# A recurrent cell of 624 steps: products in three gate blocks, a one-step loop, and one input-gate piece ahead of the choice

## The reference

```
def step(carry, x_t):
    h, c = carry
    logits = concatenate([h, c, x_t]) @ W_sel.T + b_sel
    onehot = one_hot(argmax(logits), 4)
    g_all = x_t @ W_ih[s] + h @ W_hh[s] + b_ih[s] + b_hh[s]   # for each s of 4
    i, f, g, o = split(g_all of the chosen s, 4)              # 512 each
    c = sigmoid(f) * c + sigmoid(i) * tanh(g)
    h = sigmoid(o) * tanh(c)
```

## Time and profile before

| | us |
|---|---|
| median of 3 runs | 7053.28 (7048.97 to 7054.98) |
| profiled execution | 7064.35 |
| its span | 7062.7 |
| granted TensorE clock, mean over the span | 0.956 |
| PE busy | 6163.6 (87%) |
| DVE busy | 2459.5 (35%) |
| ACT busy | 1721.2 (24%) |
| the recurrent steps in the trace | 3603.5 to 6681.9 |

### The profile page before, as it was taken

How to read it: one execution, slowest core, us unless ns; L and a number is a source line. 1 busy time by engine, 2 the same in 40 slices (tenths; PEclk the granted TensorE clock), 3 DMA queues, 4 the chain that set the end, 5 groups by cost and what they waited for, 6 DMA issues and landing times. The chain is left out here.

```text
span 7062.7 us, 492288 instructions
## 1 busy us (share of the span) xinstructions
PE 6163.6 (87%) x210539; PEld 4094.5 (58%) x210539; DVE 2459.5 (35%) x11546; ACT 1721.2 (24%) x8472; POOL 928.5 (13%) x2082
## 2 busy tenths in 40 slices
PE   6856999999999999998779999999999999999852
PEld 5523555555555454554567777777777777777631
DVE  5324555555442211111233332333333332222248
ACT  0121333333333333333001111111111111111112
POOL 0011111111128810000000000000000000000003
PEclk9977999999999999999899999999999999999975
DMA  1011111111111100000232221222122221111100
GB/s 48 1 45 35 33 34 33 34 33 34 34 35 43 42 4 0 0 0 0 76 88 41 41 41 16 41 41 44 21 32 44 41 34 7 7 7 7 22 14 8
DMA packets 806866, 204.14 MB, mean 29 GB/s; under 512 B 701431, under 2 KB 766683, under 8 KB 806804
## 3 DMA queue, kind: packets, MB, share of 16 engines
q1 hardware_dynamic: 764500, 151.79, 11.3%
q0 software_dynamic: 41152, 46.42, 2.4%
q10 hardware_dynamic: 1152, 5.15, 0.2%
HBM read 174.86 MB, written 28.16 MB: 29 GB/s over the span
## 5 line engine op out<-in xcount | busy, mean ns | idle before, releaser
L1757 PE MATMUL ps_rows<-whh,h_pair 128*4 128x320 f16 x34944 | 1307.2, 299 | 85.1 <-issue 3.4
L1074 PE MATMUL ode_busy<-ode_busy_x,ode_busy_w 128*32 128x320 f16 (+4 forms) x19248 | 1247.9, 321 | 9.3 <-PEq L1010 7.1
L1757 PEld LDWEIGHTS ps_rows<-whh,h_pair 128*4 128x4 f16 x34944 | 735.5, 84 | 512.5 <-DVE h_pair L1615 154.0
L1068 PEld LDWEIGHTS ode_psa<-ode_a,ode_w2t 128*32 128x32 f32 x19968 | 397.6, 108 | 769.1 <-ACT ode_a L1183 572.3
L1627 DVE COPY gate_rows<-ps_rows_last 128x192 f32<-128x192 f32 x624 | 223.1, 358 | 1514.3 <-PE ps_rows_last L1757 1514.3
L1193 DVE SCALAR_TENSOR_TENSOR ode_part<-ode_b 128x1 f32<-128x1 f32 x624 | 112.6, 180 | 1647.9 <-ACT ode_b L1185 1647.9
L1679 ACT COPY gate_rows<-ps_rows 128x320 f32<-128x320 f32 x624 | 265.8, 426 | 1678.8 <-PE ps_rows L1757 1678.8
L1068 PE MATMUL ode_psa<-ode_a,ode_w2t 128*32 128x1 f32 x19968 | 606.8, 181 | 47.8 <-ACT ode_a L1177 43.1
L1185 ACT ACTIVATE ode_b<-ode_psa 128x1 f32<-128x1 f32 x2496 | 427.4, 171 | 814.3 <-PE ode_psa L1068 797.6
L1801 PE MATMUL ps_gates<-l_gsel,gate_rows 128*32 128x4 f32 x19968 | 397.4, 176 | 147.4 <-DVE gate_rows L1627 147.2
L1757 PE MATMUL ps_rows_last<-whh,h_pair 128*4 128x192 f16 x19968 | 521.7, 246 | 0.0
(11 more groups left out here) (505 smaller groups left out, 9528.1 us busy)
## 6 DMA issues: line engine op xcount, KB each, us to landing
late_w<-in_wih_t SPq DMA_DIRECT2D x386, 128.0 KB, 2.1
xg_buf<-xg_scratch SPq DMA_DIRECT2D x1248, 16.0 KB, 2.0
split_raw<-in_whh_t SPq DMA_DIRECT2D x64, 256.0 KB, 2.6
ig_w<-in_wih_t SPq DMA_DIRECT2D x8, 2048.0 KB, 11.6
xg_scratch<-late_out SPq DMA_DIRECT2D x24, 624.0 KB, 3.2
whh<-h_scratch SPq DMA_DIRECT2D x90, 62.5 KB, 2.4
xg_scratch<-ig_out ACTq DMA_DIRECT2D x8, 628.0 KB, 8.2
h_scratch<-mlp_h SPq DMA_DIRECT2D x40, 125.0 KB, 2.3
```

The costliest lines, as they stand in the source:

```text
L1068: m = nc.tensor.matmul(ps[32 * j:32 * j + 32, 0:1], w[:, 32 * j:32 * j + 32], col, start=start, stop=stop, skip_group_check=True)
L1074: nc.tensor.matmul(ps_busy[32 * j:32 * j + 32, 0:cols], busy_w[:, 32 * j:32 * j + 32], busy_x[:, 0:cols], start=True, stop=True, skip_grou ...
L1757: m = nc.tensor.matmul(out[32 * j:32 * j + 4, :], hpair[:, c, 2 - 2 * part:6 - 2 * part], whh[:, at + lo:at + hi], start=(part == 0 and c ...
```

## The change

Weights and products. The recurrent weights are laid out anew on the host, so that j is a chunk of 128 hidden numbers and the streamed columns are the gates: 256 columns of the input and candidate gates (`FIRST`, to `ps_rows`, two sets in a bank), 128 of the forget gate (`ps_rows_forget`), 128 of the out gate (`ps_rows_out`). ACT copies the first block, DVE the two others one after the other. PE turns the first two gates, the forget gate, and then the out gate into a bank of its own; ACT takes tanh of the first three gates and apart from them of the out gate, and DVE makes the out gate and the gated selection weights from that.

Input gates. ACT copies them from `xg_buf` into both banks of `ps_gates` before it waits for the rows; the turns add to them.

Late pieces. PE runs one step a loop turn. One piece (slot 1) stands between the 32 products ahead and the wait for `best`, one (slot 0) at the end of the step; their chunks alternate, and the place in the input is worked out in registers in each step. They always add; DVE clears `ps_late` after each quad. DVE moves a quad after the first piece of the step after it. SP loads each chunk by itself, into the slot just read, and POOL passes on that it is there (`late_ready`). The input's share of the logits moves to the end of the step before.

```diff
+    FIRST = 2 * 128
...
+        psg = ctx.enter_context(nc.psum_tensor("ps_rows", [128, CELLS * FIRST], F32))
+        psf, pso = (ctx.enter_context(nc.psum_tensor(n, [128, BANK], F32)) for n in ("ps_rows_forget", "ps_rows_out"))
+        pscq = ctx.enter_context(nc.psum_tensor("ps_gates", [128, 2, BANK], F32))
+        psc, psq = pscq[:, 0, 0:16], pscq[:, 1, 0:16]
...
+                            gates_of_next_turn(o * TURNS + quad, 0)
+                            sp.wait_ge(S["late_used"], used + 1)
+                            load_late(2, quad)
+                            gates_of_next_turn(o * TURNS + quad, 1)
+                            sp.wait_ge(S["late_used_pre"], used + 2)
+                            load_late(3, quad)
+                            sp.wait_ge(S["late_used"], used + 2)
+                            load_late(0, quad + 1)
+                            sp.wait_ge(S["late_used_pre"], used + 3)
+                            load_late(1, quad + 1)
...
-                    nc.vector.scalar_tensor_tensor(parts[:], act[:, 0:8], 1.0, act[:, 12:20], ALU.add, ALU.mult).then_inc(S["fi"], 1)
-                    nc.vector.tensor_scalar(ok[:], act[:, 8:12], 1.0, 1024.0, ALU.add, ALU.mult).then_inc(S["o"], 1)
+                    nc.vector.scalar_tensor_tensor(parts[:], act[:, 0:2 * KC], 1.0, act[:, 2 * KC:4 * KC], ALU.add, ALU.mult).then_inc(S["fi"], 1)
                     v.wait_ge(S["fi"], k + 1)
                     nc.vector.scalar_tensor_tensor(ccur, parts[:, KC:2 * KC], 0.5, parts[:, 0:KC], ALU.mult, ALU.add).then_inc(S["c_ready"], 1)
+                    v.wait_ge(S["out_acted"], k + 1)
+                    nc.vector.tensor_scalar(ok[:], out_tanh[:], 1.0, 1024.0, ALU.add, ALU.mult).then_inc(S["o"], 1)
+                    nc.vector.scalar_tensor_tensor(wgated[:], out_tanh[:].unsqueeze(2).broadcast_to([128, KC, PAIRS]), 1.0, wsel[:, 0:KC, :], ALU.add, ALU.mult).then_inc(S["w_ready"], 1)
+
                     v.wait_ge(S["o"], k + 1)
-                    nc.vector.tensor_tensor(wgated[:], wsel[:, 0:KC, :], ok[:].unsqueeze(2).broadcast_to([128, KC, PAIRS]), ALU.mult).then_inc(S["w_ready"], 1)
-
+                    v.sem_inc(S["seen_v"], 1)
                     v.wait_ge(S["tanh_c"], k + 1)
                     nc.vector.tensor_tensor(hcur[:], ok[:], tc[:], ALU.mult).then_inc(S["h_made"], 1)
...
-                    v.wait_ge(S["rows_last"], k)
-                    nc.vector.tensor_copy(gsb[:, FIRST:D], psb[:, 0:D - FIRST]).then_inc(S["evac_v"], 1)
+                    v.wait_ge(S["rows_forget"], k)
+                    nc.vector.tensor_copy(gsb[:, 256:384], psf[:, 0:128]).then_inc(S["evac_f"], 1)
+                    v.wait_ge(S["rows_out"], k)
+                    nc.vector.tensor_copy(gsb[:, 384:512], pso[:, 0:128]).then_inc(S["evac_o"], 1)
                     cell(k)
...
-                            v.wait_ge(S["late_used"], o * (UN * TURNS) + quad * UN + UN)
+                            v.wait_ge(S["late_used_pre"], o * (UN * TURNS) + quad * UN + (UN + 1))
                             nc.vector.tensor_scalar(late_out[:, :, ds(u, 1)].rearrange("p t e -> p (t e)"), ps_late[:, 0:BLOCK], bias[:, ds(quad, 1)], scale[:, ds(quad, 1)], ALU.add, ALU.mult).then_inc(S["late_moved"], 1)
+                            v.wait_ge(S["late_moved"], o * QUADS + quad + 1)
+                            v.sem_inc(S["seen_v"], 1)
+                            nc.vector.memset(ps_late[:, 0:BLOCK], 0.0)
...
-                    nc.scalar.activation(act[:, 0:16], psc[:, 0:16], ACT.Tanh).then_inc(S["acted"], 1)
+                    nc.scalar.activation(act[:, 0:IFG], psc[:, 0:IFG], ACT.Tanh).then_inc(S["acted"], 1)
+                    a.wait_ge(S["out_gate"], k + 1)
+                    nc.scalar.activation(out_tanh[:], psq[:, IFG:16], ACT.Tanh).then_inc(S["out_acted"], 1)
...
+                            nc.scalar.copy(pscq[:, :, 0:16], xgb[:, q, e * 16:(e + 1) * 16].unsqueeze(1).broadcast_to([128, 2, 16])).then_inc(S["xg_used"], 1)
                             a.wait_ge(S["rows_first"], k)
-                            nc.scalar.copy(gsb[:, 0:FIRST], psg[:, e * BANK:e * BANK + FIRST]).then_inc(S["evac_a"], 1)
+                            nc.scalar.copy(gsb[:, 0:FIRST], psg[:, e * FIRST:(e + 1) * FIRST]).then_inc(S["evac_a"], 1)
...
+                        g.wait_ge(late_in_pre, job * (16 * UN) + (16 + 16 * q * ahead))
+                        g.sem_inc(S["late_ready"], 1)
...
+                            m = products(e, part, c, psf[:, 0:128], 256, 384, (part, c) == (0, 0))
+                    m.then_inc(S["rows_forget"], 1)
+                    for part in range(2):
+                        for c in range(KC):
+                            m = products(e, part, c, pso[:, 0:128], 384, 512, (part, c) == (0, 0))
+                    m.then_inc(S["rows_out"], 1)
...
+                def turned(out, block_no):
+
+                    for j in range(4):
+                        m = nc.tensor.matmul(out[32 * j:32 * j + 32, :], gsb[:, block_no * 128 + 32 * j:block_no * 128 + 32 * j + 32], gsel[:, int(block_no == 1), :],
+                                             start=False, stop=True, skip_group_check=True)
+                    return m
+
...
+                def late(slot, at):
+
+                    return nc.tensor.matmul(ps_late[:, 0:BLOCK], late_w[:, slot * 128:(slot + 1) * 128], xt_all[:, ds(at, BLOCK)], start=False, stop=True, skip_group_check=True)
...
+                    pe.wait_ge(S["hp_ready"], k)
+                    for c in range(AHEAD):
+                        for e in range(CELLS):
+                            first(e, 0, c)
+                    pe.wait_ge(S["late_ready"], k)
+                    late(1, late_pre_at).then_inc(S["late_used_pre"], 1)
+                    pe.wait_ge(S["best"], k)
+                    pe.sem_inc(S["seen_pe"], 1)
...
+                    pe.wait_ge(S["evac_a"], k)
+                    turned(psc[:, 0:KC], 0)
+                    turned(psc[:, 2 * KC:3 * KC], 1)
+                    pe.wait_ge(S["evac_f"], k)
+                    turned(psc[:, KC:2 * KC], 2).then_inc(S["gates"], 1)
+                    pe.wait_ge(S["evac_o"], k)
+                    turned(psq[:, IFG:16], 3).then_inc(S["out_gate"], 1)
+                    logits_of_input()
...
+                    with pe.Fori(0, UN * TURNS) as r:
+                        step(pe.snap(o * (UN * TURNS) + r + 1), pe.snap((r % UN) * (PER * N) + token), pe.snap((1 - r % UN) * (PER * N) + (token + N)))
```

More of the change, by code:

```diff
@@ L1587, in _ @@
                         gates_of_next_turn(i, g)
-                for g in range(UN):
-                    sp.wait_ge(late_in[g], 16 * (BLOCKS * QUADS + 1))
+                for loaded in (late_in, late_in_pre):
+                    sp.wait_ge(loaded, 16 * (BLOCKS * QUADS * UN + 1))
             @block.vector
@@ new lines, in _, with logits_of_input, products @@
+                nc.tensor.matmul(psq, ident[:], xg0[:], start=True, stop=True).then_inc(S["out_gate"], 1)
+                def logits_of_input():
+                    nc.tensor.matmul(psl[0:1, 0:PAIRS], xcol[:], pairs[:], start=True, stop=False, skip_group_check=True)
+                def products(e, part, c, out, lo, hi, start):
+                    for j in range(4):
+                        at = e * CELL_COLS + (part * KC + c) * GATES + j * D
+                        m = nc.tensor.matmul(out[32 * j:32 * j + 4, :], hpair[:, c, 2 - 2 * part:6 - 2 * part], whh[:, at + lo:at + hi],
+                                             start=start, stop=(part == 1 and c == KC - 1), skip_group_check=True)
+                    return m
@@ L1744, in turn_of_two, with first, recurrent @@
+                def first(e, part, c):
+                    return products(e, part, c, psg[:, e * FIRST:(e + 1) * FIRST], 0, FIRST, part == 0 and c == 0 and e % 2 == 0)
+                def recurrent(e):
+                    for part in range(2):
                         for c in range(KC):
-                            nc.tensor.matmul(psl[0:1, 0:PAIRS], ccur[:, c:c + 1], wsel[:, KC + c, :], start=False, stop=False, skip_group_check=True)
-                        pe.wait_ge(S["w_ready"], k)
-                        pe.sem_inc(S["seen_pe"], 1)
@@ L1748, in turn_of_two @@
-                        pe.wait_ge(S["tanh_c"], k)
+                            if (part, c) >= (0, AHEAD):
+                                m = first(e, part, c)
+                    m.then_inc(S["rows_first"], 1)
+                    for part in range(2):
                         for c in range(KC):
-                            m = nc.tensor.matmul(psl[0:1, 0:PAIRS], tc[:, c:c + 1], wgated[:, c, :], start=False, stop=(c == KC - 1), skip_group_check=True)
-                        m.then_inc(S["logits"], 1)
@@ L1753, in products @@
-                        def products(e, part, c, out, lo, hi):
-                            for j in range(4):
-                                at = e * CELL_COLS + (part * KC + c) * GATES + j * D
```

(12 more changed lines are left out.)

172 lines of the change are left out of this document (83 added, 89 removed).

## The result

The changed kernel takes 7198.19 us (median of 4 runs, 7195.14 to 7203.99) against 7054.13: ratio 1.0206 (95% interval 1.0193 to 1.0219), 144 us more where 77 were forecast. The profiled execution spans 7202.3 us.

A forecast was written before the change was run, and what follows sets the result against it. Bound: each step's serial chain of products, copy, turns, gate tanh, h and split. Terms 0.03 + 0.04 + 0.06 = 0.13 us a step, times 624 = 81 us, gave 7130 us; likeliest case 7085 to 7190, range 7030 to 7235.

The forecast's parts named there:

- Chain and place: Ahead of the choice of the cell: register work of 0.54 delays the choice, its first product loads at t = 1.60.
- TensorE's own 1.43: After the piece ahead of the choice: TensorE can load the next product at t = 1.43 if register work is hidden.
- At nothing: Waits and loads priced at zero, among them TensorE's wait for late_ready and for the out copy.
- Products after the choice: TensorE's products by gate: 0.66 for the first block, forget 0.45, out 0.45; in all 1.56.
- Rival (d): Products of 128 columns stay bound by weight loads, 0.081 a group: +0.39 a step, 7375 us; chance 0.05.
- T in steps without a move: Start of the gate tanh (T) at 3.59 after the step's first weight load: +0.03 a step.
- Steps with a move: VectorE's move of ps_late delays the forget copy in 192 of 624 steps, gate tanh at 3.73: +0.04 a step on average.
- h after T: Behind the gate tanh: out gate waits for its own tanh, h at 0.91 instead of 0.85: +0.06 a step.
- Rival (c): Step's end: loop edge and drains push the last logits beyond the split of h, +0.15 a step, 7230 us; chance 0.15.
- one of the signs of a slower case: At the step's end: last logits after the split of h would make the forecast wrong on the slow side.
- (a): Piece hides under the choice, register work beside the products: first product at 1.13, -0.25 a step, 6895 us; chance 0.12.
- (b): Register work costs nothing, TensorE decides: gate tanh at 3.42, 3.73 where VectorE is late; 7065 us; chance 0.17.

The follow-up runs named there:

- one-column run: Changed kernel with the piece ahead of the choice streaming one column instead of 156, register work kept: 7186.05 us, ratio 1.0183.
- the run without a piece: Changed kernel with no piece and no register work ahead of the choice, half of the late input gates' sum left out: 6948.96 us, ratio 0.9849.

## Why the prediction was right, and what it mis-sized

The sum that the runs give: products by gate, split out gate and one-step loop -92 us (6964 against 7056); a piece ahead of the choice +140 (7105 against 6964); its register work +94 (7198 against 7105). Together 142, against 144 measured; the three parts of the first term were not taken apart. The +140 is two things. In the 432 steps without a move the first product comes 0.14 later and the mean step goes from 4.79 to 4.92, 57 us; in the 192 with a move, where VectorE now waits for the piece (its move starts at 1.71 instead of 0.84), it goes from 4.77 to 5.21, 85 us. In the old layout the piece alone costs 345 us, for two reasons: the products ahead are longer (piece at 1.19, here at 0.98), and without a piece the first product stood at 1.07, here at 1.29, held by the late logits. So these are steps along one path, not prices that hold anywhere.

- Chain and place: right. The choice behind the register work sets the first product; forecast 1.60, measured 1.65 (median of the steps). The term was mis-sized at one instruction: the fused one of seven operations takes 219 ns, not 150, just above the bound of 214. A row nearer than the one of four operations was in the trace before, of six with a modulo, at the end of the first step of a turn (L1813 at 5004.2); at 109 ns it would not have warned either. TensorE's own 1.43 came out at 1.44, twice. The Trainium skill ("TensorEngine Tiling (Array Packing)", Key Properties), by which changing the tiling mode drains the TensorE, agrees with that, but no run separates a drain from the load of the piece's 128-column weights (0.30 for its two passes, at 5009.81).
- At nothing: the wait for `late_ready` ahead of the choice was rightly left out; the piece loads at 0.97, where the products ahead alone put it.
- Products after the choice: 8 groups of 128 columns take 0.50 (5011.02 to 5011.52; forecast 0.45), 6 of 256 columns 0.55 (forecast 0.66). The copy of the forget rows starts 1.33 after the first product, forecast 1.32. Rival (d), bound by loads, is out: 0.062 a group and not 0.081.
- T in steps without a move: forecast 3.59, measured 3.66 (mean 3.68), of which 0.05 from the choice.
- Steps with a move: forecast T 3.73, measured 3.82 (3.85 on average); the clearing started 0.22 behind the move, not 0.11. But this term and the next were added as if independent. Where T is late the out gate is not, so of the 0.18 later T (3.85 against 3.68) only 0.07 reached the step (5.21 against 5.14). The one-column run shows the exchange from the other side: with the move 0.15 earlier, T falls to 3.72 in these steps and the time after T rises from 1.36 to 1.44.
- h after T: forecast + 0.06 in all steps, measured + 0.10 in 432 and none in 192, 0.07 on average. That the average is so near was luck.
- Rival (c): one of the signs of a slower case did appear. In steps without a move the last logits end at T + 1.48 (median; forecast T + 1.33), behind the split of h, which ends at T + 1.41. It cost nothing here, since the choice waits longer for the register work and the next products start 0.05 behind the split as before; it is the next bound, as the run without a piece showed. (a) and (b) needed the register work for nothing; with it nearly gone the time is (b)'s 7065 plus 40, since T was 3.44 and, with a move, 3.86 in place of 3.42 and 3.73.

Of the 0.23 a step, T gives 0.16 (mean 3.73 against 3.58; forecast 0.07) and the time after T 0.07 (forecast 0.06). What was mis-sized is thus T: without a move it came 0.09 later than forecast, 0.06 of it at the choice (mean 1.66 against 1.60), and with a move 0.12 later. Direction and chain were forecast; the size, 77 us against 144, was about half.

## What to carry to other kernels

Ahead of a branch on loaded data, count the sequencer's instructions as well as the array's: modulo and index arithmetic there can be on the critical path while the array is busy. Work that was hidden at the end of a step can cost its full length in front of a choice (0.55 a step in the old layout), and what another engine does with its result moves with it: here VectorE's move of a quad. Before unrolling a loop, look at the instruction queue's row; before blaming a collision, ask what the waiting instruction names as its releaser.

## What was not expected of the hardware

A loop body that outgrew what TensorE keeps made a step 9 us longer ((12705 - 6964)/624), with instruction fetches in every turn and a granted clock of 0.57. A fused register instruction grows with its operations, though not evenly (operations as counted in the programs of the kernel before and the changed one): 42 to 46 ns for two or three, 105 to 109 for four or six, 120 for five, 219 for seven, each with 0.06 to 0.1 us of its own around it.
